# A transformer layer with a ScalarE, VectorE, GpSimd and SyncE schedule of their own beside TensorE's

## The chip, the cores and the metric

The kernel runs on one core of one Trainium2 chip. Its time is the device time of one execution in microseconds (us), the median of several runs. The engines are TensorE (PE in the rows), VectorE (DVE), ScalarE (ACT), GpSimd (POOL) and SyncE (SP), which here issues most transfers. Each engine runs its own instructions strictly in the order in which they are written, and waits for others through semaphores.

## The reference

A layer of three parts works on x, 16 batches of 128 tokens of 512 numbers, in float32. `_layernorm` has no scale or shift.

```
x = x + xattn(layernorm(x), ctx, ctx)       # 16 heads of 32; one K and one V head for all; 2048 context rows a batch
x = x + memory(layernorm(x))                # 4 heads of 128, chunks of 64; needs inv(I - A0) of a strictly lower matrix
x = x + experts(layernorm(x))               # softmax gate, best of 16 experts, 128 rows each; relu(x w1) w2

# xattn:   softmax((q Wq + bq) K^T * 32**-0.5) V, then Wo + bo, with K = ctx Wk + bk, V = ctx Wv + bv
# memory:  v = x Ww^T, rk = x / |x| per head, wk = rk shifted by one token; v_new = A v, decayed sums over tokens
```

## The kernel before

**Tiling and stages.** `attention` does the first two parts, the gate, and scatters every token's row to its expert's place in memory; `experts`, not touched, then loops over the 16 experts. `attention` is a pipeline over batches. The scores of a batch are 64 units (4 groups `g` of 4 heads by 16 key blocks `k`), and every unit is two *ticks*, so a batch is `TICKS` = 128 ticks and a group 32. Iteration `i` runs the scores of batch `i`, the preparation of batch `i+1` (or late parts of `i+2`), and the work after attention (`finish`) of batches `i-1` and `i-2`. A tick is a place in the program and no time: every engine's function walks the same loops over `i` and `t` and emits what is due at `(i, t)`. So a tick sets nothing but the order on an engine, and what an engine waits for is in its semaphores.

**One batch.** *Preparation*: normalize `xin` (`norm`, `xn`), transpose it (`xnt`), project the queries in `KV_BANK` (`qproj`), of which VectorE makes `qs`, ScalarE its rounded part `qh`, GpSimd the rest, and 12 transfers put them in `qT`. The context comes in four chunks `c`: TensorE projects one in `KV_BANK` (`kv`), ScalarE copies half of it (`kvlow`), VectorE adds both (`kvs`), ScalarE casts two parts to `kT` (`kh`), VectorE subtracts to get a third (`kl`), and TensorE transposes the values (`vt`). *Maxima*: for each group TensorE multiplies 16 products (`largest`, two banks in turn), VectorE reduces each (`mpart`), then all to `mneg`; TensorE transposes that, ScalarE copies it (`mrow`) and a transfer appends the row to `qT`. *Scores*: TensorE (two banks in turn), exponential on ScalarE (`weights`, 18 buffers), weighted values on TensorE four units at a time, sums of the weights on GpSimd (`psum`, L1033). *After attention*: `sums` on TensorE, four reciprocals on VectorE in the idle tile of x1, their product `att`, projection `x1`, normalization `xn2` (ACT), squares `ss` (ACT), `rn` (POOL), `rk` (ACT), projection V and its copy (ACT), transposes of rk, their product I, and from it the matrices XT, MT and IT on VectorE and GpSimd. Six levels then invert the matrix: Y on TensorE, masked by VectorE; Z on TensorE, subtracted from XT by VectorE; XT transposed and copied by ScalarE to X. At last x2, the gate, and the row's place, with the scatter on GpSimd (`row`).

**What sets the order.** The numbers in `STEADY`, `SECOND` and `FIRST` (preparation; the latter two for batches 1 and 0), `POST`, `LEVEL_AT`, `MAX_AT`, `MAX_TURN` and `O_COPY`. A step has one tick for all engines: when TensorE's function emits it at `t`, the others emit their part at `t` or a fixed few ticks later, for example `kvs` at `kv` + 1, `kh` at `kv` + 2 and `kl` at `kv` + 4.

Of the kernel before, what the change touches and what calls it, by code (L numbers as in the profile page):

```python
# [11 lines left out]
B, S, D = 16, 2048, 512  # L12
# [31 lines left out]
SECOND = STEADY._replace(norm=2, xn=6, xnt=11)  # L44
FIRST = Prep(norm=4, xn=6, xnt=8, qproj=[11, 12, 13, 14], qsend=19, kv=[7, 10, 16, 18], vt=[20, 22])
LOAD_AFTER, W1_AT = 4, 80

POST = dict(xb=4, sums=12, recip=[10, 12, 14, 15], att=17, x1=[18, 19, 20, 22], x1_add=22, norm2=22, xn2=26, ss=28,
            x12=25, rn=33, xn2T=34, rk=38, V=[37, 38, 39, 40], V_copy=41, rkT=42, I=45, XT1=43, X1=49, Vn=100,
            oT2=104, x2=[108, 109, 110, 111], x2_add=110, store=122, norm3=111, xn3=115, xn3T=121, lg=124, eg=126,  # L50
            oh=127, loc=132, row=136)
LEVEL_AT = [[50, 53, 56], [59, 62, 65], [68, 71, 74], [77, 80, 83], [85, 88, 90], [94, 97, 103]]
TAIL = POST["row"] + 1 - TICKS
# [40 lines left out]
def maxima_in(i, t):  # L94

    first = [(0, 0, n) for n in range(KB) if (i, t) == (-1, FIRST_MAX[n])]
    return first + [(b, g, n) for n in range(KB) for b, g in groups_at(i, t, MAX_AT[n]) if b or g]


def turns_in(i, t):  # L100

    first = [(0, 0)] if (i, t) == (-1, FIRST_TURN) else []
    return first + [(b, g) for b, g in groups_at(i, t, MAX_TURN) if b or g]
# [19 lines left out]
def attention(nc, T, w1_first, w1_in):  # L123
    with ExitStack() as ctx:
# [111 lines left out]
        def turn_read(b, use):  # L236
# [10 lines left out]
            + [(TICKS * (b + 1) + POST["sums"], b, ("s", 0)) for b in range(B)])]  # L247
# [56 lines left out]
        def _(e):  # L304
# [32 lines left out]
            for i in range(-2, B + 2):  # L337
                for t in range(TICKS if i <= B else TAIL):
# [5 lines left out]
                    for b, g in turns_in(i, t):  # L344
                        send_max(b, g)
# [8 lines left out]
                    for b, at in ((i - 2, t + TICKS), (i - 1, t)):  # L354
                        if at == POST["store"] and 0 <= b < B:
# [13 lines left out]
        def _(e):  # L369
# [131 lines left out]
            def finish(b, t):  # L501
# [3 lines left out]
                if t in POST["x1"]:  # L505
                    c = POST["x1"].index(t)
# [7 lines left out]
                    if t == POST["x1"][3]:  # L514
                        ins.then_inc(post_pe.sem, 1)
                if t == POST["xn2T"]:
# [4 lines left out]
                if t == POST["V"][0]:  # L521
# [3 lines left out]
                if t in POST["V"]:  # L525
                    ins = project(P_BANK, turned, ww, POST["V"].index(t))
                    if t == POST["V"][3]:
                        ins.then_inc(post_pe.sem, 1)
                if t == POST["rkT"]:
# [5 lines left out]
                if t == POST["I"]:  # L535
# [4 lines left out]
                if t == POST["X1"]:  # L540
# [5 lines left out]
                for lv in range(LEVELS):  # L546
                    if t == LEVEL_AT[lv][0]:
# [10 lines left out]
                    if t == LEVEL_AT[lv][1]:  # L558
# [8 lines left out]
                    if t == LEVEL_AT[lv][2] and lv < LEVELS - 1:  # L567
# [5 lines left out]
                if t == POST["Vn"]:  # L573
                    e.wait_ge(*xt_dve.at(*level(b, LEVELS - 1, 3)))
                    per_head(P_BANK, lambda h: cut(XT, h), lambda h: cut(V, h)).then_inc(late_pe.sem, 1)
                if t == POST["oT2"]:
# [4 lines left out]
                if t == POST["x2"][0]:  # L581
# [3 lines left out]
                if t in POST["x2"]:  # L585
                    ins = project(P_BANK, turned, wr, POST["x2"].index(t))
                    if t == POST["x2"][3]:
                        ins.then_inc(late_pe.sem, 1)
                if t == POST["xn3T"]:
# [4 lines left out]
                if t == POST["lg"]:  # L594
# [7 lines left out]
                if t == POST["loc"]:  # L602
# [11 lines left out]
            for i in range(-2, B + 2):  # L614
# [7 lines left out]
                for t in range(TICKS if i <= B else TAIL):  # L622
# [11 lines left out]
                    if 1 <= i <= B and t == POST["sums"]:  # L634
                        sums(i - 1)
                    for b, g, n in maxima_in(i, t):
                        largest(b, g, n)
                    for b, g in turns_in(i, t):
# [719 lines left out]
```

## Time and profile before

| What | Value |
|---|---|
| Median of 3 runs | 2139.68 us (2138.57 to 2140.3) |
| The profiled execution's own time | 2144.96 us |
| Its span, first to last instruction | 2143.2 us |
| TensorE busy | 2011.6 us, 94% |
| GpSimd busy | 1642.2 us, 77% |
| VectorE, ScalarE busy | 1261.6 us, 1098.8 us |
| Granted TensorE clock, mean | 0.98 |

`attention` takes the first four fifths of the span, `experts` the rest. All durations of instructions come from the one profiled execution. Busy time of an engine is a sum over parts with different limits; what TensorE waits for is seen only in its list of waits and the timelines.

### The profile page before, as it was taken

How to read it: one execution, taken by the hardware profiler on the slowest of the kernel's cores; microseconds unless marked ns; L12 is line 12 of the kernel's file. 1: busy time of each engine (PE TensorE's matmuls, PEld its weight loads, DVE VectorE, ACT ScalarE, POOL GpSimd, SP SyncE). 2: the span in 40 equal slices, each digit the busy share in tenths (PEclk: the TensorE clock that was granted, in tenths of full speed). 3: DMA queues.
4: the chain of work that ended last, by engine and by line, in shares of the span. 5: the costliest groups of instructions: out<-in, count | busy, mean ns of one | idle time of the engine just before them, and what ended most of it. 6: DMA issues, size and time to landing. Idle time of an engine off the chain costs nothing. (4 is left out here: it accounts for less than half of the span.)

```text
span 2143.2 us, 33309 instructions
## 1 busy us (share of the span) xinstructions
PE 2011.6 (94%) x11884; PEld 1309.8 (61%) x11884; DVE 1261.6 (59%) x2218; ACT 1098.8 (51%) x2029; POOL 1642.2 (77%) x1387
## 2 busy tenths in 40 slices
PE   7779999999999999999999999999989999999999
PEld 4335555555554555555555555564545889999998
DVE  4556767676666666676767676666663323333333
ACT  2545555656565556555565655555554233333333
POOL 0778888898989898988888898989898145555555
PEclk7889999999999999999999999999999999999999
DMA  5752131212122121212131212211200099999994
GB/s 208 221 131 75 35 87 57 80 46 74 52 73 75 45 75 55 81 36 83 43 94 43 75 44 74 70 48 33 79 16 17 6 350 355 366 352 359 356 347 177
DMA packets 105125, 262.16 MB, mean 122 GB/s; under 512 B 8576, under 2 KB 33920, under 8 KB 96256
## 3 DMA queue, kind: packets, MB, share of 16 engines
q1 hardware_dynamic: 96912, 234.92, 32.2%
q10 hardware_dynamic: 4464, 14.62, 2.4%
q0 software_dynamic: 3584, 10.49, 1.2%
q8 instruction: 95, 1.56, 0.3%
q14 instruction: 70, 0.57, 0.1%
HBM read 223.67 MB, written 25.72 MB: 116 GB/s over the span
## 5 line engine op out<-in xcount | busy, mean ns | idle before, releaser
L1033 POOL TENSOR_TENSOR psum<-psum,weights 128x512 f32<-128x512 f32 x896 | 1161.0, 1296 | 143.1 <-ACT weights L657 37.6
L827 DVE TENSOR_REDUCE mpart<-bank 128x1 f32<-128x512 f32 x1024 | 677.5, 684 | 289.1 <-PE bank L412 279.7
L657 ACT ACTIVATE weights<-bank 128x512 f32<-128x512 f32 x1024 | 594.6, 598 | 432.8 <-PE bank L425 427.0
L425 PE MATMUL bank<-qT,kT 97*128 97x512 f32 x1024 | 480.5, 477 | 20.7 <-DMA qT<-mrow 16.1
L412 PE MATMUL bank<-kT,qT 96*128 96x512 f32 x1024 | 449.8, 452 | 21.0 <-DVE mpart L827 18.9
L412 PEld LDWEIGHTS bank<-kT,qT 96*128 96x128 f32 x1024 | 198.4, 194 | 175.5 <-issue 89.6
L425 PEld LDWEIGHTS bank<-qT,kT 97*128 97x128 f32 x1024 | 196.8, 194 | 106.3 <-issue 53.8
L1285 POOL TENSOR_TENSOR w2l<-w,w2h 128x1024 fp32r<-128x1024 f32 x64 | 201.9, 3155 | 76.7 <-PE ebank L1198 55.8
L437 PE MATMUL bank<-weights,v 128*32 128x512 f32 x2048 | 255.7, 617 | 0.0
L1228 ACT ACTIVATE hh<-ebank 128x512 fp32r<-128x512 f32 x64 | 38.2, 597 | 224.2 <-PE ebank L1182 224.2
L1222 ACT CAST w2h<-w 128x2048 fp32r<-128x2048 f32 x64 | 121.5, 1898 | 44.2 <-DMA w<-in_w 42.1
L493 PE MATMUL bank<-w_first,wkv 128*64 128x512 f32 x512 | 125.5, 610 | 4.9 <-DVE kvs L860 1.5
L437 PEld LDWEIGHTS bank<-weights,v 128*32 128x32 f32 x2048 | 53.0, 111 | 125.6 <-issue 92.5
L1249 DVE TENSOR_TENSOR w2l<-w,w2h 128x1024 fp32r<-128x1024 f32 x64 | 80.5, 1257 | 71.3 <-PE ebank L1198 48.3
L1254 DVE SCALAR_TENSOR_TENSOR hl<-ebank,hh 128x512 fp32r<-128x512 f32 x64 | 44.3, 692 | 131.7 <-ACT hh L1228 131.7
L1182 PE MATMUL ebank<-dT,w_first 128*128 128x128 f32 x1024 | 120.3, 278 | 0.9 <-DVE dT L1243 0.9
L1182 PEld LDWEIGHTS ebank<-dT,w_first 128*128 128x128 f32 x1024 | 119.4, 195 | 2.4 <-issue 1.2
L1033 POOL TENSOR_TENSOR psum<-weights 128x512 f32<-128x512 f32 x64 | 81.5, 1273 | 48.9 <-ACT weights L657 48.1
L1182 PEld LDWEIGHTS ebank<-dT,w 128*128 128x128 f32 x1024 | 117.5, 192 | 1.4
L1182 PE MATMUL ebank<-dT,w 128*128 128x128 f32 x1024 | 118.2, 275 | 0.0
L1196 PE MATMUL ebank<-w2h,hh 128*128 128x512 f32 x256 | 104.3, 407 | 0.0
L385 PEld LDWEIGHTS bank<-xr,Y 128*128 128x128 f32 x640 | 77.5, 191 | 39.9 <-DVE Y L913 39.9
(168 smaller groups left out, 2743.9 us busy)
## 6 DMA issues: line engine op xcount, KB each, us to landing
w<-in_w SPq DMA_DIRECT2D x48, 2048.0 KB, 19.7
w_first<-in_ctx SPq DMA_DIRECT2D x64, 1024.0 KB, 5.2
w_first<-in_w SPq DMA_DIRECT2D x16, 2048.0 KB, 12.2
dispatched<-route ACTq DMA_DIRECT2D x17, 513.0 KB, 9.6
dis<-dispatched SPq DMA_DIRECT2D x16, 513.0 KB, 3.5
qT<-qh SPq DMA_DIRECT2D x128, 64.0 KB, 4.1
qT<-qs SPq DMA_DIRECT2D x64, 64.0 KB, 2.2
xr<-in_x SPq DMA_DIRECT2D x16, 256.0 KB, 2.8
```

Source lines behind the costliest of these rows:

```text
L412: e.matmul(a[:], qT[b % 2][0:3 * HD, (4 * g + h) * P:(4 * g + h + 1) * P], kT[b % 2][0:3 * HD, c * 512:(c + 1) * 512], start=True, stop=Tr ...
L425: e.matmul(B_BANK[u % 2][:], kT[b % 2][0:3 * HD + 1, k * P:(k + 1) * P], qT[b % 2][0:3 * HD + 1, g * 512:(g + 1) * 512], start=True, stop= ...
L437: ins = e.matmul(PV_BANK[HD * j:HD * (j + 1), :], v1[b % 2][:, k + j, :], p[(UNITS * b + u + j) % NP], start=k == 0, stop=k == KB - 4)
L493: ins = e.matmul(KV_BANK[rows, :], wkv[:, j, :], cxT[c][:, j, :], start=j < 2, stop=j >= 2)
L657: e.activation(p[n % NP], B_BANK[u % 2][:], ACT.Exp).then_inc(p_act.sem, 1)
L827: e.tensor_reduce(mpart[g % 2][:, 4 * (n % 4) + n // 4:4 * (n % 4) + n // 4 + 1], max_bank(b, g, n)[:], AX.X, ALU.max).then_inc(max_dve.se ...
L1033: e.tensor_tensor(acc[:], first, p[(UNITS * b + u) % NP], ALU.add).then_inc(psum_pool.sem, 1)
L1182: ins = e.matmul(H_BANK[g][:, f * P:(f + 1) * P], w1[q][:, c, (4 * g + f) * P:(4 * g + f + 1) * P], dT[q][:, c, :], start=c == 0, stop=c = ...
L1196: e.matmul(Y_BANK[q][:], hh[g % 2][:, part], w2h[g][:, f, :], start=k == 0, stop=False)
L1222: e.copy(w2h[g][:], w2[q][:, 4 * g:4 * g + 4, :]).then_inc(w2h_act.sem, 1)
L1249: e.tensor_tensor(w2l[g % 2][:, 0:2, :], w2[x % 2][:, 4 * g:4 * g + 2, :], w2h[g][:, 0:2, :].bitcast(F32), ALU.subtract).then_inc(w2l_dve. ...
L1285: e.tensor_tensor(w2l[g % 2][:, 2:4, :], w2[q][:, 4 * g + 2:4 * g + 4, :], w2h[g][:, 2:4, :].bitcast(F32), ALU.subtract).then_inc(w2l_pool ...
```

## The change

TensorE keeps its ticks, and its order comes out as it was. Every other engine gets ticks of its own for each step, in `ACT_AT`, `DVE_AT`, `POOL_AT`, `MAX_DVE`, and new fields of `Prep`. Their numbers say "at this place among my other work" and need no longer equal TensorE's or a fixed distance. SyncE's order comes out as it was, too.

```diff
-Prep = namedtuple("Prep", "norm xn xnt qproj qsend kv vt")
-STEADY = Prep(norm=-32, xn=-29, xnt=-27, qproj=[24, 26, 27, 29], qsend=52, kv=[18, 37, 58, 74], vt=[42, 79])
+Prep = namedtuple("Prep", "norm norm_pool xn xnt xnt_act qproj q_dve q_act q_pool qsend kv kvlow kvs kh kl vt vt_act")
+STEADY = Prep(norm=-58, norm_pool=-40, xn=-31, xnt=-27, xnt_act=-27, qproj=[24, 26, 27, 29], q_dve=30, q_act=31,
+              q_pool=30, qsend=52, kv=[18, 37, 58, 74], kvlow=[18, 37, 59, 74], kvs=[21, 38, 60, 75], kh=[23, 44,
+              65, 76], kl=[33, 89, 95, 106], vt=[42, 79], vt_act=[42, 79])
...
-POST = dict(xb=4, sums=12, recip=[10, 12, 14, 15], att=17, x1=[18, 19, 20, 22], x1_add=22, norm2=22, xn2=26, ss=28,
-            x12=25, rn=33, xn2T=34, rk=38, V=[37, 38, 39, 40], V_copy=41, rkT=42, I=45, XT1=43, X1=49, Vn=100,
...
+PE_AT = dict(sums=12, x1=[18, 19, 20, 22], xn2T=34, V=[37, 38, 39, 40], rkT=42, I=45, X1=49, Vn=100, oT2=104,
...
+ACT_AT = dict(xn2=28, ss=30, rk=38, xn2T=34, V=41, rkT=42, X1=49, Vn=100, oT2=104, xn3=116, xn3T=121, eg=126, X=[56,
+              65, 74, 83, 90])
+DVE_AT = dict(recip=[10, 12, 14, 15], att=16, x1=22, XT1=45, MT=46, IT=47, x2=110, lg=124, oh=127, row=136, Y=[50,
+              58, 68, 76, 85, 94], Z=[53, 62, 71, 80, 89, 97])
+POOL_AT = dict(xb=4, norm2=23, x12=25, rn=30, MT0=40, XT1=42, norm3=114, row=180)
...
-MAX_TURN, PV_AT = -9, [17, 17, 33, 33]
-O_COPY = 1
-
-FIRST_MAX, FIRST_TURN = [24 + n // 2 for n in range(KB)], 33
+MAX_DVE = [-39, -38, -37, -34, -32, -30, -29, -27, -24, -23, -22, -19, -15, -15, -13, -12]
+MAX_TURN, MAX_ROW, PV_AT = -9, -9, [17, 17, 33, 33]
+O_COPY = 4
...
-                if t - 2 in prep(b).kv:
-                    c = prep(b).kv.index(t - 2)
+                if t in prep(b).kh:
+                    c = prep(b).kh.index(t)
...
-                if t - 4 in prep(b).kv:
-                    c = prep(b).kv.index(t - 4)
+                if t in prep(b).kl:
+                    c = prep(b).kl.index(t)
```

How rows move is shown at three places of a steady batch. A line of the program has another number in the changed kernel (L706 is L698 of before).

ScalarE, around its copy of V. Before, the casts of kT (`kh` of chunk 1, here from kvs0) stand between rk and V:

```order
L669 COPY oS0<-bank4 128x512
L657 ACTIVATE weights<-bank3 128x512
L725 COPY turned<-bank7 128x512
L657 ACTIVATE weights<-bank2 128x512
L691 COPY kvlow<-bank6 64x512
L657 ACTIVATE weights<-bank3 128x512
L722 ACTIVATE rk<-xn2,rn 128x128 x4
L698 CAST kT0<-kvs0 32x512 x2
L657 ACTIVATE weights<-bank2 128x512
L728 COPY V<-bank7 128x512
```

ScalarE, the same place of the changed kernel:

```order
L733 COPY turned<-bank7 128x512
L665 ACTIVATE weights<-bank2 128x512
L677 COPY oS0<-bank4 128x512
L699 COPY kvlow<-bank6 64x512
L665 ACTIVATE weights<-bank3 128x512
L730 ACTIVATE rk<-xn2,rn 128x128 x4
L665 ACTIVATE weights<-bank2 128x512
L736 COPY V<-bank7 128x512
L665 ACTIVATE weights<-bank3 128x512
L712 COPY v10<-bank5 128x4x2x32
L739 COPY rkT<-bank7 128x4x128
L665 ACTIVATE weights<-bank2 128x512
L706 CAST kT0<-kvs0 32x512 x2
```

The two casts moved behind the copy of rkT, and the copy of oS0 behind that of `turned`.

VectorE, from the maximum ahead of the reciprocals (x1 is their tile) to the addition that makes x1. Before:

```order
L827 TENSOR_REDUCE mpart1<-bank0 128x1
L883 RECIPROCAL x1<-bank6 128x128
L827 TENSOR_REDUCE mpart1<-bank1 128x1
L883 RECIPROCAL x1<-bank6 128x128
L827 TENSOR_REDUCE mpart1<-bank0 128x1
L883 RECIPROCAL x1<-bank6 128x128 x2
L827 TENSOR_REDUCE mpart1<-bank1 128x1
L827 TENSOR_REDUCE mpart1<-bank0 128x1
L889 TENSOR_TENSOR turned<-bank7,x1 128x512
L860 SCALAR_TENSOR_TENSOR kvs0<-bank6,bias,kvlow 64x512
L827 TENSOR_REDUCE mpart1<-bank1 128x1
```

VectorE, the same place of the changed kernel:

```order
L835 TENSOR_REDUCE mpart1<-bank0 128x1
L835 TENSOR_REDUCE mpart1<-bank1 128x1
L891 RECIPROCAL x1<-bank6 128x128 x2
L835 TENSOR_REDUCE mpart1<-bank0 128x1
L891 RECIPROCAL x1<-bank6 128x128 x2
L897 TENSOR_TENSOR turned<-bank7,x1 128x512
L835 TENSOR_REDUCE mpart1<-bank1 128x1
L835 TENSOR_REDUCE mpart1<-bank0 128x1
L835 TENSOR_REDUCE mpart1<-bank1 128x1
L835 TENSOR_REDUCE mpart1<-bank0 128x1
L842 TENSOR_REDUCE mneg<-mpart1 128x4
L868 SCALAR_TENSOR_TENSOR kvs0<-bank6,bias,kvlow 64x512
```

One maximum moved ahead of the first reciprocal, the product (`turned`) ahead of two maxima, and `kvs0` behind the last two maxima and `mneg`.

VectorE, level 4 of the inverse (Y is masked, `xr` is XT, from which Z is subtracted). Before:

```order
L834 TENSOR_REDUCE mneg<-mpart1 128x4
L913 TENSOR_TENSOR Y<-bank7,cst 128x512
L827 TENSOR_REDUCE mpart0<-bank0 128x1
L927 TENSOR_TENSOR xr<-xr,bank7 128x512
L827 TENSOR_REDUCE mpart0<-bank1 128x1
```

VectorE, the same place of the changed kernel:

```order
L842 TENSOR_REDUCE mneg<-mpart1 128x4
L921 TENSOR_TENSOR Y<-bank7,cst 128x512
L874 TENSOR_TENSOR kT1<-kvs0,kT1 32x512
L835 TENSOR_REDUCE mpart0<-bank0 128x1
L935 TENSOR_TENSOR xr<-xr,bank7 128x512
L835 TENSOR_REDUCE mpart0<-bank1 128x1
```

A subtraction for kT (`kl` of chunk 1) now stands between Y and Z.

## Rows read from the trace of the kernel before

**Rows 1.** The page: its head, and part 1, busy time of each engine.
```profile
span 2143.2 us, 33309 instructions
PE 2011.6 (94%) x11884; PEld 1309.8 (61%) x11884; DVE 1261.6 (59%) x2218; ACT 1098.8 (51%) x2029; POOL 1642.2 (77%) x1387
```
**Rows 2.** Windows: busy us of PE, PEld, DVE, ACT, POOL; clock; DMA.
```profile
500.00:600.00 100.00, 95.10 (x544) 54.97 (x544) 68.66 (x124) 58.29 (x119) 88.00 (x81) 1.00 0.21 64
```
**Rows 3.** Waits of TensorE, whole span: us in total, times, longest.
```profile
PE bank L412 <- DVE mpart L827: 18.9, 36, 1.1
PE bank L377 <- ACT V L728: 17.6, 15, 1.3
PE bank L417 <- DVE mneg L834: 17.0, 19, 1.8
PE bank L425 <- DMA qT<-mrow: 16.1, 2, 10.2
```
**Rows 4.** Timeline of ScalarE: start, duration, what, [idle before <- releaser].
```profile
589.77 1.28 ACT L722 ACTIVATE rk<-xn,rn 128x128 f32<-128x128 f32 x4 [1.10 <-POOL rn L1064]
591.07 1.26 ACT L698 CAST kT<-kvs 32x512 fp32r<-32x512 f32 x2
...
592.85 0.58 ACT L728 COPY V<-bank 128x512 f32<-128x512 f32 x1
```
**Rows 5.** Timeline of TensorE in the same steady stretch.
```profile
509.29 0.94 PE L385 MATMUL bank<-xr,Y 128*128 128x128 f32 x6 [0.20 <-DVE Y L913]
...
532.40 0.66 PE L571 MATMUL bank<-cst,xr 128*128 128x128 f32 x4 [0.28 <-DVE xr L927]
...
562.09 1.06 PE L459 MATMUL bank<-psum,cst 128*32 128x512 f32 x8
...
565.64 0.50 PE L412 MATMUL bank<-kT,qT 96*128 96x512 f32 x1 [0.72 <-DVE mpart L827]
...
568.80 1.51 PE L493 MATMUL bank<-w_first,wkv 128*64 128x512 f32 x6 [0.15 <-DVE x L883]
...
575.48 1.05 PE L479 MATMUL bank<-xnT,wq 128*128 128x128 f32 x8
...
593.48 0.66 PE L377 MATMUL bank<-cst,rk 128*128 128x128 f32 x4 [1.26 <-ACT V L728]
```
**Rows 6.** Timeline of GpSimd in that stretch.
```profile
527.88 4.12 POOL L1033 TENSOR_TENSOR psum<-psum,weights 128x512 f32<-128x512 f32 x3 [1.18 <-ACT weights L657]
...
538.86 1.27 POOL L1033 TENSOR_TENSOR psum<-weights 128x512 f32<-128x512 f32 x1 [0.16 <-ACT weights L657]
...
548.97 0.19 POOL L1036 TENSOR_TENSOR rs<-mv,eps 128x1 f32<-128x1 f32 x1 [0.30 <-DVE rs L874]
...
550.01 11.22 POOL L1033 TENSOR_TENSOR psum<-psum,weights 128x512 f32<-128x512 f32 x8
```
**Rows 7.** Timeline of VectorE in that stretch (x is x1's tile, xr is XT).
```profile
507.91 0.73 DVE L860 SCALAR_TENSOR_TENSOR kvs<-bank,bias,kvlow 64x512 f32<-64x512 f32 x1
...
531.66 0.69 DVE L927 TENSOR_TENSOR xr<-xr,bank 128x512 f32<-128x512 f32 x1 [0.44 <-PE bank L385]
...
564.08 0.96 DVE L883 RECIPROCAL x<-bank 128x128 f32<-128x128 f32 x1 [0.68 <-PE bank L459]
...
568.57 1.22 DVE L827 TENSOR_REDUCE mpart<-bank 128x1 f32<-128x512 f32 x2
...
573.39 0.69 DVE L827 TENSOR_REDUCE mpart<-bank 128x1 f32<-128x512 f32 x1 [0.63 <-PE bank L412]
```
**Rows 8.** kT's subtraction (200 to 1500 us) and GpSimd's additions: duration ns min/median/max.
```profile
L866 DVE TENSOR_TENSOR kT<-kvs,kT x52: 680/681/1059, 210.1 to 1492.9; 32x512 fp32r<-32x512 f32 x52
...
L1033 POOL TENSOR_TENSOR psum<-psum,weights x896: 1259/1274/1677, 55.5 to 1654.3; 128x512 f32<-128x512 f32 x180
```
**Rows 9.** Timeline of TensorE, the first batch and batch 15's iteration.
```profile
69.08 0.33 PE L417 MATMUL bank<-cst,mneg 128*128 128x128 f32 x1 [1.81 <-DVE mneg L834]
...
1580.74 0.77 PE L425 MATMUL bank<-qT,kT 97*128 97x512 f32 x1 [2.10 <-ACT weights L657]
```

More of the change, by code:

```diff
@@ new lines @@
+ACT_AT = dict(xn2=28, ss=30, rk=38, xn2T=34, V=41, rkT=42, X1=49, Vn=100, oT2=104, xn3=116, xn3T=121, eg=126, X=[56,
[3 more added lines that the diff above has]
+POOL_AT = dict(xb=4, norm2=23, x12=25, rn=30, MT0=40, XT1=42, norm3=114, row=180)
+STORE = 122
+TAIL = max(PE_AT["loc"], ACT_AT["eg"], DVE_AT["row"], POOL_AT["row"], STORE) + 1 - TICKS
@@ L91, in prep, with maxima_in, turns_in @@
     return (FIRST, SECOND)[b] if b < 2 else STEADY
-def maxima_in(i, t):
+def maxima_in(i, t, at):
     first = [(0, 0, n) for n in range(KB) if (i, t) == (-1, FIRST_MAX[n])]
-    return first + [(b, g, n) for n in range(KB) for b, g in groups_at(i, t, MAX_AT[n]) if b or g]
-def turns_in(i, t):
+    return first + [(b, g, n) for n in range(KB) for b, g in groups_at(i, t, at[n]) if b or g]
+def turns_in(i, t, at):
     first = [(0, 0)] if (i, t) == (-1, FIRST_TURN) else []
-    return first + [(b, g) for b, g in groups_at(i, t, MAX_TURN) if b or g]
+    return first + [(b, g) for b, g in groups_at(i, t, at) if b or g]
 def quads_in(i, t):
@@ L246, in attention @@
             + [(TICKS * (b - 1) + prep(b).qproj[0], b, ("q", 0)) for b in range(B)]
-            + [(TICKS * (b + 1) + POST["sums"], b, ("s", 0)) for b in range(B)])]
+            + [(TICKS * (b + 1) + PE_AT["sums"], b, ("s", 0)) for b in range(B)])]
         def kv_read(b, use):
@@ L343, in _ @@
                             send_queries(b)
-                    for b, g in turns_in(i, t):
+                    for b, g in turns_in(i, t, MAX_ROW):
                         send_max(b, g)
@@ L354, in _ @@
                     for b, at in ((i - 2, t + TICKS), (i - 1, t)):
-                        if at == POST["store"] and 0 <= b < B:
+                        if at == STORE and 0 <= b < B:
                             e.wait_ge(*late_dve.at(b, "x2"))
@@ L566, in finish @@
                             ins.then_inc(z_pe.sem, 1)
-                    if t == LEVEL_AT[lv][2] and lv < LEVELS - 1:
+                    if lv < LEVELS - 1 and t == PE_AT["XT"][lv]:
                         for i, bk, hs in parts:
@@ L633, in _ @@
                         weigh(b, u)
-                    if 1 <= i <= B and t == POST["sums"]:
+                    if 1 <= i <= B and t == PE_AT["sums"]:
                         sums(i - 1)
-                    for b, g, n in maxima_in(i, t):
+                    for b, g, n in maxima_in(i, t, MAX_AT):
                         largest(b, g, n)
-                    for b, g in turns_in(i, t):
+                    for b, g in turns_in(i, t, MAX_TURN):
                         turn_max(b, g)
@@ L709, in finish @@
                 banks = banks_of(b)
-                if t == POST["xn2"]:
+                if t == ACT_AT["xn2"]:
                     e.wait_ge(*post_pool.at(b, "nb2"))
                     normalize(xn2[:], x1[:], rs2).then_inc(post_act.sem, 1)
-                if t == POST["ss"]:
+                if t == ACT_AT["ss"]:
                     e.wait_ge(*post_act.at(b, "xn2"))
@@ L801, in _ @@
                         out_sum(*done)
-                    for b, g in turns_in(i, t):
+                    for b, g in turns_in(i, t, MAX_ROW):
                         max_row(b, g)
@@ L852, in prepare @@
                         q_dve.sem, 1)
-                if t - 1 in prep(b).kv:
-                    c = prep(b).kv.index(t - 1)
+                if t in prep(b).kvs:
+                    c = prep(b).kvs.index(t)
                     e.wait_ge(*kvlow_act.at(b, c))
@@ L886, in finish @@
                         e.tensor_tensor(cut(turned, h), cut(P_BANK, h), cut(recip, h), ALU.mult).then_inc(o_dve.sem, 1)
-                if t == POST["att"] and b < LAST:
+                if t == DVE_AT["att"] and b < LAST:
                     e.wait_ge(*recip_done(b, 3))
                     e.tensor_tensor(turned[:], P_BANK[:], recip[:], ALU.mult).then_inc(o_dve.sem, 1)
-                if t == POST["x1_add"]:
+                if t == DVE_AT["x1"]:
                     e.wait_ge(*post_pe.at(b, "x1"))
@@ L951, in finish @@
                         late_dve.sem, 1)
-                if t == POST["row"]:
+                if t == DVE_AT["row"]:
                     e.wait_ge(*late_pe.at(b, "loc"))
@@ L1000, in _ @@
                         prepare(i + 2, t - TICKS)
-                    for b, g, n in maxima_in(i, t):
+                    for b, g, n in maxima_in(i, t, MAX_DVE):
                         largest(b, g, n)
@@ L1064, in finish @@
                     e.tensor_tensor(rn[:], rn[:], mhalf[:], ALU.pow).then_inc(post_pool.sem, 1)
-                if t == POST["rkT"]:
+                if t == POOL_AT["MT0"]:
                     e.wait_ge(*post_pool.at(b, "x12"))
```

131 lines of the change are left out of this document (66 added, 65 removed).

## The prediction

> **What bounds the kernel now.** I read the page first: TensorE is busy for 94% of the span, GpSimd for 77%, VectorE and ScalarE for little over half [rows 1]. The windows then split the span. Between 200 and 1500 us the kernel repeats one pattern, a batch per 100 us; in one such window TensorE is busy 95.10 us, GpSimd 88.00 us, and the granted clock is full [rows 2]. So a batch has 4.9 us in which TensorE stands still. The change can win those and little else: TensorE's own order and its instructions stay. The list of its waits names who is late: maxima of VectorE 18.9 us in all, ScalarE's copy of V 17.6 us in 15 waits, VectorE's negated maximum 17.0 us, and two waits for the transfer of the maximum row, 16.1 us together, both in the first batch [rows 3]. Last I read the timelines around those waits, and asked of each whether the late instruction was slow, or stood behind something that could have come later. Only the second kind can go.
>
> **The change part by part, for one steady batch.**
>
> *V.* ScalarE is idle 1.10 us for GpSimd's rn, scales rk until 591.05, casts kT for 1.26 us, does an exponential, and copies V from 592.85 on [rows 4]. TensorE waits 1.26 us for that copy [rows 5]. The change puts the two casts behind the copy of rkT, and rn on GpSimd ahead of one more addition (a step of 1.42 us, from 11.22 us for 8, less their overlap) [rows 6]. The casts alone give back 1.26 us. What becomes late next is the projection that V is copied from, which is TensorE's own. I take all that the run shows: 17.6 us in 15 waits, of which fourteen of about 1.25 make up 17.5 (the fifteenth is short: its iteration has no casts). Bounds: 0 (if V stays late by the queue of exponentials) and 1.26. In their new place, behind the copy of rkT, the casts delay the next exponential. TensorE does not need that one until two scores on, since the scores have two banks. I cost that at nothing; without this cover it would be the casts' 1.26 us again.
>
> *Reciprocals.* VectorE sits idle 0.68 us for the sums; then come four reciprocals with two maxima between them, two more maxima from 568.57 on, and the product (att) [rows 7]. TensorE waits 0.72 us for the maximum behind the first reciprocal and 0.15 us for the last reciprocal [rows 5]. Now a maximum stands ahead of the first reciprocal, in the idle 0.68 us (it takes 0.61, half of the 1.22 us row), so the first wait goes. The reciprocals end 0.61 us sooner, and the context projection at 568.80 starts by that much sooner: 0.6 us gained, not the 0.87 us of both waits. Bounds 0 and 0.87. The product moves ahead of two maxima, which their banks allow: TensorE fills the next one after 1.92 us of weighted sums.
>
> *Level 1 of the inverse.* Y is masked behind kvs, which takes 0.73 us from 507.91 on; TensorE waits 0.20 us for it [rows 5, 7]. Y now goes first: 0.2 us gained. kvs comes behind Y and a maximum, 1.3 us later; its reader, ScalarE's cast, stands two exponentials later than before: 0.
>
> *kT subtractions (kl).* Three of the four move to ticks 89, 95 and 106. The one at 89 lands between Y and Z of level 4. Z already ends last there: TensorE waits 0.28 us for it [rows 5]. VectorE is idle 0.44 us before Z, which starts at 531.66 [rows 7]. This takes most of a subtraction of 0.68 us, the median, but not one of 1.06 us, the longest [rows 8]. Loss 0.24 us at the median, 0.62 at the most, and 0 if the maximum before Z can start sooner, too; I take 0.2. At the other two places VectorE has longer gaps, and the reader, a maximum's matmul, comes ten ticks or more behind the subtraction: 0.
>
> *kvs of chunk 0* moves behind two maxima and mneg. The last of these starts at 573.39, after a wait for TensorE itself [rows 7]. So kvs ends near 573.39 + 0.69 + 0.2 + 0.73 = 575.0, or 574.4 with the 0.6 us above. The query projection, which overwrites the bank that it reads, stands at 575.48, 574.9 then [rows 5]. Margin 0.5 us: no cost, but the thinnest place; x1's addition, queued behind, gains instead from the subtraction that left.
>
> *GpSimd.* The scatter's issue moves 44 ticks on; nothing waits for it before the next batch's x2, 58 ticks later. The scaling steps (rs3, rs2) go one addition later, where GpSimd idled 0.30 us for VectorE [rows 6]. xn2 and its squares on ScalarE go behind an exponential each. The transposes that read them stand six ticks behind xn2's new place. The statistics of xin go 26 ticks earlier, GpSimd's part of them 8, and their input has landed by then. Cost of all of these: nothing; their cover is that ScalarE works 58.29 us in 100 and VectorE 68.66 [rows 2]. Without it, each is a step of 0.6 to 1.4 us.
>
> *Transfer queue and first batch.* SyncE's order comes out the same row for row. In the first batch mneg is late by 1.81 us [rows 9], since kvs stood ahead of two maxima and waited for ScalarE; this mostly goes, but the row that it feeds then meets a wait for the transfer of up to 10.2 us [rows 3]. I take 1.2 us, bounds 0 and 4 (with the shorter waits for maxima there). The second half of the first preparation is spread over later ticks, yet its maxima start with the queries' arrival, as before: 0.
>
> *Batch 15's iteration*, without preparation, has its own waits; the longest is 2.10 us for an exponential queued behind xn2 [rows 9]. The exponential now goes first, but the next one waits on the same GpSimd result. I take 1.4 us, bounds 0 and 3.
>
> **Sum.** 1.25 + 0.6 + 0.2 - 0.2 = 1.85 us a batch; 14 batches give 25.9; with 1.2 and 1.4, 28.5 us. The profiled execution took 2144.96 us, for a span of 2143.2; it would take 2116.5. It lies 5.3 us above the median of the three runs, 2139.68, to which I apply the same difference: 2111.2, **2111 us**.
>
> **A rule weighed.** The subtraction reads two tiles of SBUF. It takes 680 to 1059 ns in the steady part, and GpSimd's additions, mostly 1.27 us, reach 1.68 us [rows 8]: the two engines do delay each other by up to 0.4 us. The sum takes 0.2 us for it, on VectorE alone, and leaves 1.85 us a batch. The Trainium skill, "GPSIMD Engine Reference", section 1 (Specifications), says that GpSimd shares its SBUF interfaces with VectorE and contends with instructions that have two SBUF inputs. The trace agrees (0.4 us), and the rule speaks against the new places: every subtraction put where GpSimd never pauses is paid twice. By it a batch keeps between 0.85 and 1.85 us, as rival 2 works out from rows.
>
> **Rivals.**
>
> 1. *The V term fails*: V's copy stays as late, by rn or by an exponential. For it: ScalarE does idle 1.10 us for rn [rows 4]. Against: rn also moves earlier, by 1.42 us. Only 28.5 - 17.5 = 11 us remain: 2129. Chance 0.07.
>
> 2. *GpSimd takes over at the sums.* From 527.88 to 561.23 it works with pauses of 0.16 and 0.30 us alone [rows 6], and the sums, at 562.09, need its last addition [rows 5]; room 0.8 us. Three subtractions now fall into this run. At 0.4 us each they add 1.2 us; less the two pauses 0.74, which the room just takes. If VectorE's statistics meet it too, or a meeting costs twice this, a batch loses up to 1.0 us: 2111 to 2125, typically 2120. The Trainium skill's "GPSIMD Engine Reference", as above, is about this meeting. Chance 0.2.
>
> 3. *Slower: kvs of chunk 0 is late.* If it comes later than the query projection by more than 0.5 + 1.8 us, each batch loses more than it wins. At 3 us more delay than I worked out, the loss is 0.65 us by 14, 9 us: 2149. Against: the last maximum ahead waits for TensorE itself, so it can't drift that far. Chance 0.05.
>
> 4. *More*: an earlier VectorE also shortens the mneg and remaining maxima waits, and transfers in the first batch land sooner by what they start sooner. Half of mneg's 17.0 us: 2103. Chance 0.12.
>
> 5. *Nothing*: the slack is taken up elsewhere, 2140, 0.03.
>
> **How the numbers follow.** The forecast holds 0.53, its own range 2105 to 2117. Taking in rival 2, part of 4 and the start's bounds, 2101 to 2124 holds 8 in 10. A measurement here tells 0.2% (4.3 us) from no change: faster takes the forecast, rivals 1, 2 and 4, 0.92; same 0.03; slower 0.05.
>
> **What would show it.** TensorE's wait for V gone in 14 batches; the wait of 0.72 us at the first reciprocal gone, and a wait for the last reciprocal of 0.2 to 0.3 us in its place; the wait for Z of level 4 grown to 0.4 or 0.5; mneg's 0.8 us unchanged; TensorE near 96.9 us busy in 100, GpSimd near 90; batches 98.2 us apart. New waits of the sums for GpSimd's additions would show rival 2; of the query projection for kvs, rival 3.

## The result, and the profile after

The changed kernel takes 2108.02 us (median of 4 runs, 2106.23 to 2109.55), the kernel before 2139.99 us (4 runs, 2138.57 to 2140.38). The ratio is 0.9851, with a 95% interval of 0.9834 to 0.9869: 28 to 35.5 us faster, 32.0 by the medians. The forecast was 2111 us in a range of 2101 to 2124. The profiled executions lie further apart, 2144.96 and 2107.52 us.

The page of the changed kernel, its head and part 1, against [rows 1]:

```profile
span 2105.7 us, 33309 instructions
PE 1997.6 (95%) x11884; PEld 1311.0 (62%) x11884; DVE 1272.6 (60%) x2218; ACT 1092.2 (52%) x2029; POOL 1640.3 (78%) x1387
```

The windows of one steady batch (the columns are those of [rows 2]):

```profile
486.30:583.77 97.47, 94.13 (x544) 55.19 (x544) 69.36 (x124) 57.93 (x118) 87.90 (x81) 1.00 0.23 66
```

A batch takes 97.47 us for 100.03. TensorE's idle time fell from 4.9 to 3.3 us, and its busy time by 1 us too, with the same 544 instructions at the same clock. What that second part comes from is taken up below.

The waits of TensorE in that batch, and below them the largest of the whole span, against [rows 3]:

```profile
PE bank L425 <- DVE mneg L842: 0.8, 1, 0.8
PE bank L501 <- DVE x L891: 0.5, 1, 0.5
PE bank L579 <- DVE xr L935: 0.5, 1, 0.5
PE bank L393 <- ACT xn L742: 0.4, 1, 0.4
PE bank L393 <- DVE Y L921: 0.3, 1, 0.3
PE bank L420 <- DVE mpart L835: 0.3, 1, 0.3
...
PE bank L425 <- DVE mneg L842: 16.2, 19, 1.2
PE bank L433 <- DMA qT<-mrow: 11.6, 3, 5.5
PE bank L579 <- DVE xr L935: 7.9, 15, 0.5
PE bank L501 <- DVE x L891: 7.6, 14, 0.6
PE bank L420 <- DVE mpart L835: 6.9, 21, 1.0
```

The wait for V is gone from the batch. That for the last reciprocal (x, L891) stands at 0.5 us for 0.15, that for Z (xr, L935) at 0.5 for 0.28, and the maxima fell from 18.9 us in 36 waits to 6.9 in 21.

TensorE's order is the same row for row in both kernels, so the two traces can be laid on each other, and the lead of the changed one read at every matmul. In the batch from the V of 593.48 us to that of 693.52 us of before, the lead grows by 2.6 us, in these steps:

```
V                              -1.41     predicted -1.25
Y, level 1                     -0.36               -0.2
Y, level 3                     -0.17                0
Z, level 4                     +0.21               +0.2
maxima at the first reciprocal -0.87 }
context projection             +0.39 } -0.58       -0.6 with its small steps
small steps, together          -0.3
```

From the first sums (161.82 and 158.18 us) to the sums of batch 13 (1462.57 and 1425.58) it grows by 33.35 us in 13 batches, 2.57 each.

### The profile page after: what moved, and what is told of

Same layout as the page of the kernel before. It is cut to its first block and busy times, and to the rows that moved or that the text cites. A ratio compares the mean times of both kernels' runs of the same rounds, so it can differ in the third digit from the quotient of the medians.

```text
span 2105.7 us, 33309 instructions
## 1 busy us (share of the span) xinstructions
PE 1997.6 (95%) x11884; PEld 1311.0 (62%) x11884; DVE 1272.6 (60%) x2218; ACT 1092.2 (52%) x2029; POOL 1640.3 (78%) x1387
## 5 line engine op out<-in xcount | busy, mean ns | idle before, releaser
L420 PEld LDWEIGHTS bank<-kT,qT 96*128 96x128 f32 x1024 | 198.0, 193 | 159.2 <-DVE mpart L835 79.6
L1299 POOL TENSOR_TENSOR pad<-pad 128x1 f32<-128x1 f32 x16 | 15.9, 995 | 109.3 <-issue 102.4
```

The costliest lines, as they stand in the source:

```text
L420: e.matmul(a[:], qT[b % 2][0:3 * HD, (4 * g + h) * P:(4 * g + h + 1) * P], kT[b % 2][0:3 * HD, c * 512:(c + 1) * 512], start=True, stop=Tr ...
```

## The experiments

All kernels below are the program of the changed kernel, with its own numbers or those of the kernel before, and a few of them set otherwise. So line numbers are the changed kernel's, in "the kernel before" with an edit, too; TensorE's and SyncE's orders stay row for row. Each was timed in turn with the kernel before, whose median in these four sets of runs was 2144.4, 2144.9, 2144.3 and 2142.2 us.

| Kernel | Median, us | Ratio to before, 95% interval | Steady batch, us |
|---|---|---|---|
| casts_alone | 2197.53 | 1.0253 (1.0240 to 1.0266) | 103.5 to 104.8 |
| rn_alone | 2139.52 | 0.9982 (0.9969 to 0.9995) | 99.7 |
| sums_alone | 2146.23 | 1.0007 (0.9993 to 1.0021) | 100.3 |
| casts_and_kl1 | 2173.71 | 1.0149 (1.0127 to 1.0170) | 102.5, the first four 100.9 to 106.8 |
| kl_back | 2228.86 | 1.0401 (1.0378 to 1.0423) | 103.3 to 106 |
| kl_soon_norm3 | 2147.00 | 1.0013 (0.9999 to 1.0027) | 98.9 to 101.1 |
| core_only | 2129.51 | 0.9936 (0.9918 to 0.9955) | 99.3 |
| xt_back | 2107.21 | 0.9836 (0.9817 to 0.9856) | 97.5 |
| first_back | 2110.70 | 0.9842 (0.9824 to 0.9861) | 97.5 |
| norm3_back | 2105.36 | 0.9820 (0.9801 to 0.9838) | 97.4 |
| recip_last | 2120.24 | 0.9875 (0.9854 to 0.9896) | 97.9, but one of 102.7 |
| one_extra | 2111.89 | 0.9854 (0.9832 to 0.9876) | 97.5 |

### One part alone

**casts_alone.** The kernel before, and

```diff
-kh=[20, 39, 60, 76]
+kh=[20, 44, 60, 76]
```

> The kernel before with one number changed: ScalarE's casts of kT's chunk 1 stand behind the copy of rkT (tick 44 for 39); everything else, GpSimd's rn too, at its old place. Theory A (the casts alone keep V waiting, and a wait of TensorE that goes gives back its listed idle time and some 0.16 us more): the wait of 1.26 us for V is gone in 14 batches, each 1.42 us shorter, 20 us in all: 2120 us, steady batches 98.6 us apart. Theory B (only the listed idle time comes back): 17.5 us, 2122.5, batches 98.8 us apart. Theory C (ScalarE stays late by rn or by the exponential ahead of V): the wait stays above 0.5 us, 2130 or more.

No theory foresaw 53 us more. VectorE's timeline has the reason, and TensorE's wait from the same batch stands below it:

```profile
605.27 0.68 DVE L874 TENSOR_TENSOR kT<-kvs,kT 32x512 fp32r<-32x512 f32 x1 [3.97 <-ACT kT L706]
...
PE bank L420 <- DVE mpart L835: 4.4, 3, 3.4
```

The subtraction for kT (tick 41) reads what the casts write. With the casts put behind the copy of rkT it stands on VectorE and waits for them 3.97 us, two maxima queued behind it, and TensorE waits 3.4 us for a maximum. The wait for V is gone, as theory A said, and more than it was worth is paid elsewhere: in that batch 1.42 us are won at V, 3.57 us lost at the maximum, and 2.4 us more in the matmuls behind it, where the granted clock is 0.50 between 606 and 612 us. So the move of that subtraction to tick 89, in which the prediction saw a cost only, is what permits the move of the casts.

**rn_alone.** The kernel before, with rn=30 for 33.

> The kernel before with one number changed: GpSimd's rn goes three ticks earlier (30 for 33), ahead of one more addition; the casts stay between rk and V. Theory A (the wait for V has two causes in a row on ScalarE, 1.10 us of idling for rn and 1.26 us of casts, and either one is enough to end it almost): rk starts up to 1.10 us sooner, TensorE's wait for V falls to 0.1 or 0.2 us, 14 x 1.1 = 15 us: 2124 us. Theory B (the exponential between the casts and V, and the projection, hold V where it is): less than 0.4 us a batch, 2134 or more. Theory C (the moved rn makes the sums or x12 late): slower than 2140.

The wait for V falls from 1.26 to 0.04 us, so either cause was enough, as theory A has it. But the batch is 0.3 us shorter, not 1.1: laid on the trace of before, TensorE gains 1.22 us at V and gives back 0.29 at the next maximum, 0.27 at the transposes of XT, for which GpSimd is now late by 0.11 us, and 0.38 at Z of level 1. These steps had had TensorE's own lateness as their cover. At the maximum and at Z there is a second cause: the subtractions for kT that stand ahead of them on VectorE take longer. In the kernel before (first two rows) and in rn_alone:

```profile
592.36 0.68 DVE L866 TENSOR_TENSOR kT<-kvs,kT 32x512 fp32r<-32x512 f32 x1 [1.18 <-ACT kT L698]
610.34 1.06 DVE L866 TENSOR_TENSOR kT<-kvs,kT 32x512 fp32r<-32x512 f32 x1 [0.50 <-ACT kT L698]
...
583.20 1.53 DVE L874 TENSOR_TENSOR kT<-kvs,kT 32x512 fp32r<-32x512 f32 x1
601.61 1.46 DVE L874 TENSOR_TENSOR kT<-kvs,kT 32x512 fp32r<-32x512 f32 x1 [0.50 <-ACT kT L706]
```

The 0.40 us more of the second is what Z of level 1 loses; why a subtraction can take twice its time is worked out under kl_soon_norm3. Theory B has the size and not the reason.

**sums_alone.** The kernel before, with the maxima n = 10 and 12 one tick earlier and later on VectorE, and the product earlier:

```diff
-MAX_DVE = [... -23, -21, -19, -16, -15, ...]   att=17
+MAX_DVE = [... -23, -22, -19, -15, -15, ...]   att=16
```

> The kernel before with VectorE's order around the sums alone changed: one maximum goes ahead of the first reciprocal, the product ahead of two maxima. Theory A (the reciprocals' end sets the context projection): the wait of 0.72 us at the first reciprocal gone, the wait for the last reciprocal 0.5 us for 0.15, so 0.5 to 0.65 us a batch, 15 batches, 8 to 10 us: 2131 us. Theory B (both waits go): 0.87 us and more a batch, 13 us and more: 2127 or less. Theory C (VectorE is late elsewhere by as much, for example in mneg): 2138 or more.

At the sums it goes as theory A says: -0.89, and +0.39 at the context projection. A Y of level 3, now behind one more maximum, gives back 0.36 us, and an exponential 0.5. The latter is a chain over three engines: the subtraction of chunk 0, ahead of x1's addition, takes 1.17 us here, the statistics and GpSimd's scaling come later, ScalarE idles 2.12 us for xn2 and has an exponential queued behind it, and TensorE waits 0.34 us for that.

```profile
679.80 1.17 DVE L874 TENSOR_TENSOR kT<-kvs,kT 32x512 fp32r<-32x512 f32 x1 [0.57 <-ACT kT L706]
681.00 0.69 DVE L901 TENSOR_TENSOR x<-bank,xr 128x512 f32<-128x512 f32 x1
...
684.63 0.81 ACT L680 ACTIVATE xn<-x,rs 128x512 f32<-128x512 f32 x1 [2.12 <-POOL rs L1048]
```

The changed kernel has that subtraction behind (tick 33) and xn2 behind the exponential.

**casts_and_kl1.** The kernel before, with kh[1] = 44 and kl[1] = 89, to see the term for V with its missing half.

> The kernel before with two numbers changed: the casts of kT's chunk 1 behind the copy of rkT (44 for 39), as in casts_alone, and VectorE's subtraction that waits for them moved along (89 for 41). Theory A (casts_alone lost its 100 us because VectorE's subtraction, left at its place, waited 4 us for the casts and held the maxima; with it out of the way the term for V is whole): V's wait gone, 1.2 to 1.4 us a batch, 14 batches, 17 to 20 us faster: 2122 to 2125 us. Theory B (as rn_alone: what V's wait gives back, waits for level 1, XT and maxima take again, as long as VectorE's other steps keep their places): V's wait gone, but batches only 0.3 to 0.6 us shorter, 2133 to 2138.

(casts_alone had lost 53 us, not the 100 of this expectation.) V's wait is gone (-1.42), VectorE waits for no late cast, and the batch is still 2.5 us longer: +0.60 at XT (GpSimd late by 0.43 us), +0.4 at Z of level 1 (behind a subtraction of 1.42 us, as in rn_alone), +1.14 at a maximum, and 1.6 us at the matmuls behind it. VectorE's subtraction and TensorE at that place:

```profile
636.32 1.58 DVE L874 TENSOR_TENSOR kT<-kvs,kT 32x512 fp32r<-32x512 f32 x1
...
638.67 0.50 PE L420 MATMUL bank<-kT,qT 96*128 96x512 f32 x1 [0.99 <-DVE mpart L835]
...
640.37 3.14 PE L445 MATMUL bank<-weights,v 128*32 128x512 f32 x16
```

and the windows around it (busy us of the engines, then the granted clock):

```profile
638.60:641.00 2.40, 2.33 (x19) 1.31 (x23) 2.34 (x5) 0.61 (x2) 2.11 (x3) 0.99 0.03 7
641.00:643.00 2.00, 2.00 (x14) 0.22 (x4) 1.11 (x5) 0.00 (x0) 1.74 (x4) 0.50 0.00 0
643.00:644.50 1.50, 1.50 (x13) 0.98 (x9) 0.00 (x0) 0.58 (x1) 0.00 (x0) 0.55 0.00 0
```

The subtraction takes 1.58 us, not the 0.68 that its place was costed with, the three maxima behind it are late, and behind the wait of 0.99 us TensorE runs at half its clock (0.50, the 1.2 GHz level) for some 3 us.

### Back from the changed kernel

**kl_back.** The changed kernel, with kl=[22, 41, 62, 78].

> The changed kernel with the four subtractions for kT back at their old distance from the projections. Theory A (the subtraction between Y and Z of level 4 is what lengthened the wait for Z from 0.28 to 0.53 us, and the old places cost nothing): 14 x 0.22 = 3 us faster than the changed kernel, 2105 us. Theory B (the old places delay other maxima or Y and Z of the levels 1 and 2 by 0.1 to 0.3 us each, which is why they were free to move): the Z wait back at 0.28 us, but others appear; 2107 to 2112. Theory C (GpSimd's additions are what counts, and the places decide how often the two engines meet): the sums' last addition shifts by over 0.3 us, time either way by up to 5 us.

The same wait as in casts_alone: 3.91 us of VectorE for the casts, 3.41 of TensorE. The subtraction of chunk 2 (tick 62, its casts at 65) waits for its casts, too, and TensorE then 1.91 us for Z of level 1. Z's wait of level 4 does return to 0.30 us. VectorE at chunk 2, and the windows behind the wait of 3.41 us, which show what it cost beyond itself:

```profile
635.83 0.68 DVE L874 TENSOR_TENSOR kT<-kvs,kT 32x512 fp32r<-32x512 f32 x1 [2.15 <-ACT kT L706]
...
615.70:617.00 1.30, 1.28 (x5) 1.18 (x6) 1.01 (x2) 0.00 (x0) 0.00 (x0) 0.50 0.06 13
617.00:619.00 2.00, 2.00 (x9) 1.68 (x8) 0.99 (x3) 0.32 (x1) 0.00 (x0) 0.50 0.00 0
...
621.00:622.00 1.00, 1.00 (x12) 0.12 (x4) 0.00 (x0) 0.00 (x0) 0.86 (x2) 1.00 0.00 0
```

From 615.7 to about 621 the granted clock is 0.50, and what the batch loses grows from 3.57 us at the wait to 5.85 us at 621.0. In the batches of 103.3 to 103.6 us the granted clock stays 1.00. Here and in casts_alone my expectations missed the same dependency.

**kl_soon_norm3.** The changed kernel, with kl=[25, 46, 67, 78], each two ticks behind its casts, and the third normalization back as in norm3_back below.

> norm3_back with the four subtractions for kT each two ticks behind its casts, as they were before (25, 46, 67, 78 for 33, 89, 95, 106), so that no subtraction stands between Y and Z of level 4 and none waits for a cast that comes later. Theory A (kl_back lost its 120 us only to the wait for the late cast; the place between Y and Z costs 0.22 us a batch): no long wait on VectorE, Z's wait back at 0.28 us, 3 us faster than norm3_back: 2102 us. Theory B (the old distance puts a subtraction ahead of x1's addition and the steps of level 1 again, and these are late by its 0.7 us and more): new waits for an exponential behind xn2 or for XT, 0.3 to 0.8 us a batch, 2108 to 2118.

Neither theory. No subtraction stands between Y and Z of level 4, but one at 616.56 starts just behind an addition of GpSimd. VectorE, GpSimd and TensorE at that place, each from its own timeline:

```profile
616.56 1.70 DVE L874 TENSOR_TENSOR kT<-kvs,kT 32x512 fp32r<-32x512 f32 x1
618.29 0.69 DVE L835 TENSOR_REDUCE mpart<-bank 128x1 f32<-128x512 f32 x1
618.90 0.68 DVE L921 TENSOR_TENSOR Y<-bank,cst 128x512 f32<-128x512 f32 x1
...
616.43 1.27 POOL L1041 TENSOR_TENSOR psum<-psum,weights 128x512 f32<-128x512 f32 x1
...
617.67 1.71 POOL L1041 TENSOR_TENSOR psum<-weights 128x512 f32<-128x512 f32 x1
...
619.63 0.38 PE L393 MATMUL bank<-xr,Y 128*128 128x128 f32 x1 [1.99 <-DVE Y L921]
```

The addition ends at 617.70, the subtraction 0.56 us later, and the next addition takes 1.71 us for 1.27. Y, behind the subtraction and a maximum, is 1.99 us late. Records of other places say the same; "rest" is what the addition that was running still had to do when the subtraction started:

```
kernel             rest   subtraction took
changed            0.14   0.69
changed            0.43   0.98
changed            0.86   1.41
casts_and_kl1      1.03   1.58
kl_soon_norm3      1.14   1.70
```

Its duration is the rest and 0.55 us, and never under 0.68. In all the traces together, the 363 such subtractions with a rest over 0.3 us took the rest and 0.54 to 0.55 us, and the 271 that started with no GpSimd instruction running took 0.68. So it does not run beside an addition, it stands until that one ends, and an addition issued meanwhile is longer, by 0.44 us here and by up to 0.5 us elsewhere. The Trainium skill, "SBUF — State Buffer", section "SBUF: two separate sides", says that VectorE's instructions with two SBUF inputs and GpSimd's lock a shared pair of ports for the whole instruction, whoever starts first. The traces agree, with the numbers above.

**core_only.** The changed kernel, with all the moves back that the prediction costed at nothing on ScalarE and GpSimd, VectorE's statistics of xin among them, and the numbers of the first two batches:

```diff
-norm=-58, norm_pool=-40, xn=-31, q_pool=30   xn2=28, ss=30, xn3=116   O_COPY = 4
+norm=-32, norm_pool=-32, xn=-29, q_pool=33   xn2=26, ss=28, xn3=115   O_COPY = 1
-norm2=23, MT0=40, XT1=42, norm3=114, row=180   kvlow=[18, 37, 59, 74]
+norm2=22, MT0=42, XT1=43, norm3=111, row=136   kvlow=[18, 37, 58, 74]
```

> The changed kernel with all the steps back at their old places that the prediction costed at nothing on ScalarE and GpSimd: xn2 and its squares, both other normalizations, kvlow, the queries' rest, the copies of the groups' outputs, MT and XT's parts, the scatter, and the first batch's numbers. VectorE's table, the casts and subtractions for kT and rn stay changed. Theory A (those moves cost and bring nothing in a steady batch; the gain is in VectorE's table, the casts and rn): steady batches 97.5 us apart as in the changed kernel, 2108 to 2112. Theory B (as sums_alone showed, an exponential queued behind xn2 is what waits next): TensorE waits 0.3 us and more for an exponential once a batch, batches 97.9 or more apart, 2115 to 2120.

The steady batch is 99.3 us: these moves carry 1.8 of the 2.6 us. Laid on the trace of before, the terms for V, Y and the reciprocals are all there (-1.39, -0.30, -0.95 and +0.29), and given back are 0.83 us at XT, 0.53 at a maximum, and 0.2 each at two scores. The largest, TensorE and then GpSimd:

```profile
588.00 0.66 PE L385 MATMUL bank<-cst,xr 128*128 128x128 f32 x4 [0.72 <-POOL xr L1081]
...
585.44 1.29 POOL L1041 TENSOR_TENSOR psum<-psum,weights 128x512 f32<-128x512 f32 x1
586.67 1.27 POOL L1081 TENSOR_TENSOR xr<-xr,cst 128x512 f32<-128x512 f32 x1
...
557.02 1.12 POOL L1091 DMA_INDIRECT dispatched<-route,sidx  x1 [0.17 <-issue]
```

In the changed kernel GpSimd comes to this step so early that it waits 1.01 us for VectorE. The second loss has two causes on VectorE, ahead of the maximum that is late:

```profile
624.27 1.50 DVE L874 TENSOR_TENSOR kT<-kvs,kT 32x512 fp32r<-32x512 f32 x1
625.81 0.69 DVE L849 BATCH_NORM_STATS2 st<-xin 128x6 f32<-128x512 f32 x1
...
626.94 0.69 DVE L835 TENSOR_REDUCE mpart<-bank 128x1 f32<-128x512 f32 x1
```

The subtraction takes 1.50 us where the same one takes 0.98 in the changed kernel (over all of them the median is 1499 ns in core_only, 882 in the changed kernel, 681 before), and behind it stand the statistics of xin, 1.1 us, which the changed kernel has at tick -58 and which are back at -32 here. No run separates the two. Theory A falls, and theory B has the direction but neither the size nor the cause; its exponential is the smallest part.

**xt_back.** The changed kernel, with MT0=42, XT1=43: was that move the cover of V's term?

> The changed kernel with two numbers of GpSimd's table back (MT0 42 for 40, XT1 43 for 42), so that one addition of the weights stands again ahead of its part of XT. Theory A (this move, costed at nothing in the prediction, is what lets the term for V arrive: with V in time TensorE comes to XT's transposes 1.4 us sooner, and GpSimd's part, one addition of 1.42 us later, is late): a new wait of TensorE for GpSimd of 0.4 to 0.7 us in 14 batches, each 0.6 to 0.85 us longer, 8 to 12 us slower than the changed kernel: 2116 to 2120 us, batches 98.2 us apart. Theory B (GpSimd idles 1.0 us for VectorE at that place, so an addition there is nearly free): under 0.3 us a batch, 2108 to 2112.

Theory B. The step now ends at 583.86, TensorE comes to it at 584.21, and nothing waits. What also lay ahead of it in core_only is the scatter of the batch before: its issue takes 1.12 us of GpSimd, and at tick 136 it stands ahead of x12 and rn, at tick 180 behind this step. So GpSimd had two moves of over a microsecond there, and this one can be missed. That the scatter's move is what suffices is inferred from these rows; it was not run apart from the other moves.

**first_back.** The changed kernel with the numbers of the first batch as before.

> The changed kernel with the first batch's own numbers (preparation, maxima) as before; the steady batches stay changed. Theory A (most of what the start gained, 3.6 us at the first sums, comes from the first batch's own places): 2110 to 2112 us, first sums near 161 us. Theory B (the start's gain comes from the steady numbers that act on the first batch too, or from transfers that happened to land sooner): 2108 us as the changed kernel, first sums near 158 us.

Undecided: 0.9842 against 0.9851, and first sums at 159.2 us. The reason is that the start differs from one execution to the next by more than the term: over the traces of all kernels here with the old numbers of the first batch, the first sums lie between 153.5 and 165.6 us; with the new ones between 158.2 and 165.2. The waits for the maximum row's transfer go from 5.7 to 19.6 us among the former.

**norm3_back.** The changed kernel, with norm3=111, xn3=115.

> The changed kernel with the third normalization back: GpSimd's part at tick 111 for 114, ScalarE's xn3 at 115 for 116. Theory A (their later place is what makes TensorE wait 3.75 us for ScalarE in the last iteration, where few scores are left to cover it, and costs nothing elsewhere): 3 to 4 us faster than the changed kernel, 2104.5 us, that wait gone. Theory B (the late place bought something in the steady batches, since GpSimd idled for VectorE there): the wait goes, but each steady batch is 0.1 to 0.3 us longer; 2106 to 2109. Theory C (the wait of the last iteration has another cause, the additions queued on GpSimd): it stays over 2 us, 2108.

The wait for xn3 in the last iteration (route, L680) falls from 3.75 us to 0.9 at most, and a new one of 3.14 us stands just ahead of it:

```profile
1606.46 0.50 PE L433 MATMUL bank<-qT,kT 97*128 97x512 f32 x1 [3.14 <-ACT weights L665]
```

The exponential of that score is now queued behind xn3, which waits 2.34 us for GpSimd's scaling, behind its additions: theory C's cause, in theory A's place. At the sums that follow it leads by 1.15 us. The ratio 0.9820 is the best of all, but its interval meets that of the changed kernel; a gain is not shown.

**recip_last.** The changed kernel, with both maxima ahead of the reciprocals:

```diff
-MAX_DVE = [... -24, -23, -22, -19, ...]   recip=[10, 12, 14, 15]
+MAX_DVE = [... -24, -23, -23, -19, ...]   recip=[9, 10, 11, 12]
```

> The changed kernel with VectorE's two maxima at the sums both ahead of the four reciprocals, which then follow one another. Theory A (the maximum between the second and the third reciprocal is all that keeps the context projection waiting 0.54 us): that wait shrinks by the maximum's 0.61 us, the second maximum still in time; 0.5 to 0.7 us a batch, 15 batches, 8 to 10 us faster than the changed kernel: 2099 us. Theory B (the two maxima don't both fit into the idle time ahead of the sums, since the second one's product comes only then): the first reciprocal starts that much later, no gain or a loss, 2107 to 2113. Theory C (gained here and lost to GpSimd, which is late at the sums): a wait of the sums for GpSimd's last addition appears.

Context projection -0.60, as theory A; but the maximum behind the four reciprocals (3.39 us) is 1.06 us late. So a maximum has to stand in their middle. One batch takes 102.7 us: its granted clock is 0.50 from 836.6 to 846.8 us, with no wait of TensorE ahead of it but the 0.82 us for mneg that every batch has. Part of this kernel's time is that, and not the maxima.

```profile
651.90 3.39 DVE L891 RECIPROCAL x<-bank 128x128 f32<-128x128 f32 x4
655.21 0.63 DVE L835 TENSOR_REDUCE mpart<-bank 128x1 f32<-128x512 f32 x1
```

**one_extra.** The changed kernel, with one more addition a batch on GpSimd, of 1.03 us in the row below:

```diff
+if t == 5:
+    e.tensor_tensor(x12[:], bo[:], bo[:], ALU.add)
```

> The changed kernel with one more addition a batch on GpSimd (128x512, some 1.27 us, into the tile x12, which is rewritten before anything reads it), placed behind xb ahead of the sums. Theory A (GpSimd is nearly the bound: it works without a pause from a third of the batch before to the sums, and its last addition ends 0.77 us before them): a wait of the sums for GpSimd of about 1.42 - 0.77 = 0.65 us a batch and 0.1 to 0.2 us for the reload, 15 batches, 10 to 12 us slower than the changed kernel: 2119 us. Theory B (GpSimd has hidden room, as its busy share of 88 us in 97.5 says): within 2 us of 2108.

Theory B: the steady waits of TensorE are those of the changed kernel, and GpSimd is busy 89.3 us of 97.5.

```profile
554.27 1.03 POOL L1111 TENSOR_TENSOR x<-bo 128x512 f32<-128x512 f32 x1
```

My expectation had put the addition on the wrong side of its deadline: in the program it comes behind the last addition that the sums need, and the pauses of GpSimd later in the batch take it up. Whether the 0.77 us of room ahead of the sums would hold against one more addition there was not tried.

## Why the prediction was right, and where its steps were wrong

**V.** The mechanism and the place are right: 1.26 us of wait gone in 14 batches, nothing late behind it. rn_alone shows that rn or the casts each would do. The size was 1.25 and is 1.39 to 1.44 us. Rival 1 falls.

**The listed wait is not the whole price.** TensorE's busy time fell by 1 us a batch, too. Where nothing waits, a matmul starts before the one ahead has ended. The transposes at V of the changed kernel, against the last row of [rows 5]:

```profile
577.03 0.60 PE L385 MATMUL bank<-cst,kvs 128*128 128x128 f32 x4
577.47 0.60 PE L385 MATMUL bank<-cst,rk 128*128 128x128 f32 x4
```

577.03 + 0.60 is 577.63, so the second group starts 0.16 us inside the first. In the trace before, the idle time is counted from the end of the first, and the overlap is lost besides. Each wait that went gave 0.1 to 0.2 us more than its row: V 1.41 for 1.26, the maximum 0.87 for 0.72, Y 0.36 for 0.20. That is about half a microsecond of the 0.7 by which 1.85 us a batch was too little, and about half of the fall of the busy time. The other half is in steps with no listed wait in either kernel, Y of level 3 and the small steps of the table; no run shows what they come from. The profile models where matmuls end, so the split of a step into idle and busy time is rough; the leads are differences of starts.

**Reciprocals, Y, Z.** 0.58 for 0.6 us, 0.36 for 0.2, and a loss of 0.21 for 0.2, with Z's wait at 0.53 us as forecast. The sign given for the last reciprocal, a wait of 0.2 to 0.3 us, was not met: it is 0.54 us, and the sum came out since the first reciprocal gave back more than its row. Of the rivals, kvs of chunk 0 was late nowhere in the steady batches, mneg's waits stayed (16.2 us in all for 17.0), and nothing took the slack.

**The step that failed** is "Cost of all of these: nothing; their cover is that ScalarE works 58.29 us in 100 and VectorE 68.66". The time came out right since the whole change was run; the reason is wrong. A share of busy time covers no step. GpSimd's part of XT was covered by TensorE's lateness at V, and once that was gone it was late by 0.11 us in rn_alone, 0.43 in casts_and_kl1 and 0.72 in core_only; core_only puts these moves at 1.8 of the 2.6 us a batch. The price named for the missing cover, 0.6 to 1.4 us a step, does hold the 0.83 measured. The same goes for the subtractions: the prediction has them as a loss of 0.2 us, and with them back, kl_back is 4% slower than the kernel before.

**GpSimd and VectorE.** Rival 2 had their meeting at 0.4 us on average. It costs the subtraction 0 to 1.1 us, by where in an addition it starts, and the case of the changed kernel is mild (median 0.88 us). Three kernels in which it meets the additions otherwise (core_only, casts_and_kl1, kl_soon_norm3) show 1.5 to 1.7 us (median or single record), and lose 0.5 to 2.7 us a batch behind it, in core_only with the statistics' part and in casts_and_kl1 with the clock's. The rival's place, the sums, did not become the bound: GpSimd's last addition ends 0.77 us before them, where it ended 0.86 us before them in the kernel before.

**The sum.** Start 3.6 us (forecast 1.2, and nothing to be read from one trace, as first_back shows), 13 steady batches 33.35 and the next 2.2 (25.9), the last iteration -0.6 instead of +1.4 (the new wait of 3.75 us for xn3), `experts` -1: 37.4 us between the profiled executions, where 28.5 was forecast. The profiled execution was missed by 9.0 us (2116.5 forecast, 2107.5 measured). The median came within 3.2 us since the other correction was wrong the opposite way: I took the profiled execution as 5.3 us above the kernel's time, and that of the changed kernel lies 0.5 us below its median; for the kernel before, the 58 later runs have medians of 2142.2 to 2144.9 us. That these errors cancelled is luck. By medians alone the gain is 32.0 us.

## What to carry to other kernels

Where every engine has an order of its own, a step moved later has to take its readers along, and a wait removed has to be followed to what stands next on every engine: the waits behind it are covered by the one that you remove. Of twelve kernels here that take a part of this change, add to it or take a part away, four kept its gain whole, and two parts that looked good by a row of their own made the kernel 2.5 and 1.5% slower. Read cover off the timeline, between the end of the step and the start of its reader, less what the reader will come sooner, and not off shares of busy time.

## What the runs showed of the hardware

A VectorE subtraction with two SBUF inputs stands until the GpSimd addition that is running ends: 0.68 to 1.80 us for the same 32x512 elements, the rest of the addition and 0.55 us. So the time of such a step depends on where in an addition it starts, and a move of a step on another engine can double it, as in rn_alone.

What TensorE's clock does behind a wait differs. In casts_and_kl1 a wait of 0.99 us was followed by some 3 us at half the clock (0.50) in eleven batches and by none in three; waits of 1.26 us in the kernel before, with the granted clock 1.00 over the batch, were not; of fourteen waits of 2.0 us in kl_soon_norm3 three were (at 321, 721 and 1120 us); behind the 3.4 us of kl_back the clock was 0.50 for 5 us in the batch shown, and in three of the fourteen batches not at all; and in recip_last it was 0.50 for 10 us once, behind a wait of 0.82 us. What decides is open.
